# A two-layer adaLN transformer kernel: its beginning rearranged, and a maxima lead of 40 units for 46

## The reference

```python
q = qkv[..., :2 * Hx].reshape(Bx, 2 * NQ, Sx, HD)      # 32 query heads, 8 key heads
scores = where(causal, einsum('bhqd,bhkd->bhqk', q, k) / sqrt(HD), -inf)
aw = softmax(scores).reshape(Bx, NQ, 2, Sx, Sx)
attn = einsum('bhqk,bhkd->bhqd', aw[:, :, 0] - lam * aw[:, :, 1], v) * (1 - LAMBDA_INIT)
```

## Time and profile before

| | |
|---|---|
| Median of 3 runs | 2183.7 us (2183.66 to 2185.52) |
| The profiled execution's own time | 2184.72 us |
| Its span | 2183.0 us |
| Busy share of the span: TensorE, VectorE, ScalarE, GpSimd | 94%, 80%, 70%, 32% |
| Mean granted clock of TensorE | 0.973 of 2.4 GHz |
| Beginning, to the first maxima matmul | 0 to 66.07 us |
| Lead, to the first score matmul | to 115.41 us |
| 16 groups | to 1794 us |
| Layer 0's end and layer 1 | to 2183 us |

### The profile page before, as it was taken

The page is one execution under the profiler, slowest core; times in us unless marked ns, Lnnn a source line. Parts: engine busy times, 40 slices in busy tenths (PEclk is TensorE's granted clock), DMA queues, the critical chain, the costliest instruction groups (busy, mean ns, idle before and its releaser), DMA issues. The chain is left out here.

```text
span 2183.0 us, 44397 instructions
## 1 busy us (share of the span) xinstructions
PE 2043.1 (94%) x16332; PEld 890.0 (41%) x16332; DVE 1739.4 (80%) x3954; ACT 1523.4 (70%) x3113; POOL 693.0 (32%) x1246
## 2 busy tenths in 40 slices
PE   6799999999999999999999999999999998978896
PEld 5233333333333333333333333333333327855674
DVE  2888888888888888888888888888888926833688
ACT  2068787878787878787878778787867784523564
POOL 2213232414141414232333323242311213410577
PEclk9599999999999999999999999999999998989998
DMA  5230404040303131212222221312120003110111
GB/s 150 41 70 10 74 7 74 7 73 10 70 15 65 23 58 27 53 33 48 37 43 45 36 50 30 53 28 52 29 47 24 9 2 97 39 48 1 30 49 49
DMA packets 138229, 93.09 MB, mean 43 GB/s; under 512 B 90784, under 2 KB 127776, under 8 KB 138016
## 3 DMA queue, kind: packets, MB, share of 16 engines
q1 hardware_dynamic: 138016, 90.30, 20.4%
HBM read 31.00 MB, written 20.97 MB: 24 GB/s over the span
## 5 line engine op out<-in xcount | busy, mean ns | idle before, releaser
L758 ACT ACTIVATE probs<-b_bank 128x512 f32<-128x512 f32 (+1 forms) x2304 | 1172.4, 577 | 347.2 <-PE b_bank L918 336.4
L635 DVE TENSOR_REDUCE m_part<-a_bank 128x1 f32<-128x512 f32 (+3 forms) x2048 | 1190.1, 634 | 153.8 <-PE a_bank L888 109.8
L918 PE MATMUL b_bank<-q_pack,k_pack 34*128 34x512 bf16 (+7 forms) x5120 | 920.8, 347 | 3.9 <-DMA q_pack<-m_rows 2.2
L888 PE MATMUL a_bank<-k_pack,q_pack 64*128 64x512 bf16 (+3 forms) x2560 | 810.7, 357 | 54.8 <-DVE m_part L635 31.6
L960 PE MATMUL acc<-probs,v_tile 128*32 128x512 f32 (+3 forms) x5120 | 587.4, 540 | 3.1 <-POOL probs L501 0.8
L918 PEld LDWEIGHTS b_bank<-q_pack,k_pack 64*128 64x128 bf16 (+1 forms) x5120 | 310.3, 94 | 510.6 <-ACT probs L758 436.5
L888 PEld LDWEIGHTS a_bank<-k_pack,q_pack 64*128 64x128 bf16 x2560 | 226.0, 94 | 344.6 <-DVE m_part L635 210.6
L501 POOL TENSOR_SCALAR_AFFINE_SELECT probs<-probs 128x512 f32<-128x512 f32 (+1 forms) x192 | 152.2, 793 | 608.1 <-ACT probs L758 608.0
L632 DVE CUSTOM_DVE_ANT_0 a_bank<-a_bank,mask_a 128x128 f32<-128x128 f32 (+3 forms) x512 | 241.7, 512 | 66.8 <-PE a_bank L888 66.8
L960 PEld LDWEIGHTS acc<-probs,v_tile 128*32 128x32 f32 x5120 | 107.9, 108 | 175.5 <-issue 118.5
L516 POOL TENSOR_TENSOR o_w<-o_rl,signs 128x16 f32<-128x16 f32 x64 | 14.8, 232 | 413.6 <-DVE o_rl L658 413.6
(11 more groups left out here) (210 smaller groups left out, 1756.3 us busy)
## 6 DMA issues: line engine op xcount, KB each, us to landing
q_pack<-part SPq DMA_DIRECT2D x384, 64.0 KB, 2.3
k_pack<-part SPq DMA_DIRECT2D x192, 64.0 KB, 2.3
headT<-scratch SPq DMA_DIRECT2D x80, 128.0 KB, 4.0
scratch<-qkvT SPq DMA_DIRECT2D x16, 512.0 KB, 3.0
xg<-in_L_attn_x SPq DMA_DIRECT2D x16, 256.0 KB, 2.7
scratch<-qkvT SPq DMA_DIRECT2D x32, 128.0 KB, 2.9
q_pack<-m_rows SPq DMA_DIRECT2D x256, 2.0 KB
x<-in_L_attn_x SPq DMA_DIRECT2D x4, 1024.0 KB, 9.2
```

The costliest lines, as they stand in the source:

```text
L635: dve.tensor_reduce(out, bank[:, 0:w], AX.X, ALU.max).then_inc(a_maxed, 1)
L758: act.activation(probs[:, n % P_RING, h, at:C], b_bank[bank_no(("B", n, h))][:, at:C], ACT.Exp, scale=HD ** -0.5) \
L888: ins = pe.matmul(a_bank[at % A_RING][:, 0:w], q_pack[buf][rows, hp, 0, q:q + P], k_pack[buf][rows, 0, C * c:C * c + w], start=True, stop= ...
L918: ins = pe.matmul(b_bank[bank_no(slot)][:, at:at + C - q], k_pack[par][rows, n2, P * kt:P * (kt + 1)], q_pack[par][rows, h // 2, n2, C * j ...
```

## The change

LEAD goes from 46 to 40. On GpSimd the first power comes ahead of most constants. The 36 DMAs of the first packing are divided: SyncE issues those of side 0, ScalarE those of side 1, each behind the same conditions; later groups keep all on SyncE. The row modulations leave their place before the lead: their twelve halves follow units 13, 14, 16, 17, 19, 20, 29, 30, 32, 33, 35 and 36, and ScalarE copies them. The lambda computation moves up on VectorE and ScalarE.

```diff
@@ constants @@
-LEAD = 46
+LEAD = 40
...
+MODS_AT = {u + w: (n, w) for n, u in enumerate((13, 16, 19, 29, 32, 35)) for w in range(2)}
@@ new helpers @@
+        def part_made(p):
+
+            return ((part0_ready, PIECES), (rest_ready, 2 * ROUND_AT), (parts_ready, 1))[p]
+
+        def pack_part(queue, buf, p, sides):
+
+            for n2 in range(2):
+                for r, (pq, pk) in enumerate(zip(PARTS_Q[n2], PARTS_K[n2])):
+                    for side in sides:
+                        at = HALF * side + HD * r
+                        if pk == p:
+                            queue.dma_start(k_pack[buf][at:at + HD, n2, :], part[p][HD * QH:HD * (QH + 1), :]).then_inc(packs_in, 16)
+                        for h in range(side, QH if pq == p else 0, 2):
+                            queue.dma_start(q_pack[buf][at:at + HD, h // 2, n2, :], part[p][HD * h:HD * (h + 1), :]).then_inc(packs_in, 16)
@@ SyncE, pack(n, buf, steps_done) @@
                 for p in range(3):
                     if steps_done is None:
-                        sp.wait_ge(*((part0_ready, PIECES), (rest_ready, 2 * ROUND_AT), (parts_ready, 1))[p])
-                    for n2 in range(2):
...
+                        sp.wait_ge(*part_made(p))
+                    pack_part(sp, buf, p, range(2) if steps_done is not None else (0,))
@@ GpSimd: inverse_deviation and its call for 0 moved up, behind mask_a's select @@
+            def inverse_deviation(n):
...
+            inverse_deviation(0)
             made(pool.memset(pick[:, :, :], 0.0))
...
-            inverse_deviation(0)
             inverse_deviation(1)
@@ GpSimd, pair(n) @@
                 if n == 0:
                     pool.wait_ge(lam_step, 7)
+                    pool.wait_ge(mod_taken, len(ROW_MODS))
@@ VectorE: row copies out; the lambda block moved from behind them to behind centre(1) @@
             centre(1)
+            dve.wait_ge(lam_inputs, 64)
+            dve.tensor_tensor(products, lam_in[:, 0:4:2, :], lam_in[:, 1:4:2, :], ALU.mult).then_inc(lam_step, 1)
...
-            for n in range(6):
-                dve.wait_ge(mod_ready, upto(3 + n))
-                _, b, _, at = ROW_MODS[n]
-                dve.tensor_copy(rowmod[:, at:at + 2, b, :],
-                                (b_bank[0], acc)[n % 2][:, :].rearrange("p (w d) -> p w d", w=2)).then_inc(mod_taken, 1)
@@ ScalarE @@
+            act.wait_ge(lam_step, 2)
+            act.activation(lam[:, 2:4], lam[:, 0:2], ACT.Exp).then_inc(act_consts, 1)
             for i in range(PIECES):
                 first_part(0, i)
-            act.wait_ge(lam_step, 2)
-            act.activation(lam[:, 2:4], lam[:, 0:2], ACT.Exp).then_inc(act_consts, 1)
+            act.wait_ge(pool_consts, POOL_CONSTS)
+            for p in range(3):
+                act.wait_ge(*part_made(p))
+                pack_part(act, 0, p, (1,))
+
+            def take_row_mod(n):
+
+                act.wait_ge(mod_ready, 3 + n)
+                _, b, _, at = ROW_MODS[n]
+                act.activation(rowmod[:, at:at + 2, b, :], (b_bank[0], acc)[n % 2][:, :].rearrange("p (w d) -> p w d", w=2), ACT.Copy) \
+                    .then_inc(mod_taken, 1)
+
             take_maxima(0, N_PRO - 1)
+            for n in range(2):
+                take_row_mod(n)
             for i in range(PIECES):
                 first_part(1, i)
+            take_row_mod(2)
             take_maxima(1, N_PRO)
+            for n in range(3, 6):
+                take_row_mod(n)
@@ TensorE: the loop over ROW_MODS ahead of the lead becomes row_mod(n, w) @@
+            def row_mod(n, w):
+
+                layer, b, cols, _ = ROW_MODS[n]
+                if n >= 2 and w == 0:
+                    pe.wait_ge(mod_taken, n - 1)
+                for kc in range(2):
+                    ins = pe.matmul((b_bank[0], acc)[n % 2][:, D * w:D * (w + 1)], cSb[:, layer, kc, b, :],
...
@@ TensorE, in the loop over the lead's units @@
                     turn_maxima(m)
-
+                if u in MODS_AT:
+                    row_mod(*MODS_AT[u])
+
+            pe.wait_ge(mod_taken, len(ROW_MODS))
             pe.wait_ge(m_copied, len(NEXT))
```

More of the change, by code:

```diff
@@ L425, in _ @@
                                     pattern=[[-1, P]], channel_multiplier=1))
+            def inverse_deviation(n):
+                pool.wait_ge(stats_ready, upto(n + 1))
+                if not (isinstance(n, int) and n == 0):
+                    pool.wait_ge(xhat_ready, upto(n))
+                pool.tensor_tensor(rstd[:, :], veps[:, :], expo[:, 0:2], ALU.pow).then_inc(rstd_ready, 1)
+            inverse_deviation(0)
             made(pool.memset(pick[:, :, :], 0.0))
@@ L454, in _ @@
             pool.wait_ge(pool_consts, POOL_CONSTS)
[L456 to L460, removed]
             def split(n, i):
@@ L586, in _ @@
             centre(1)
+            dve.wait_ge(lam_inputs, 64)
+            dve.tensor_tensor(products, lam_in[:, 0:4:2, :], lam_in[:, 1:4:2, :], ALU.mult).then_inc(lam_step, 1)
+            dve.wait_ge(lam_step, 1)
+            dve.tensor_reduce(lam[:, 0:2], products, AX.X, ALU.add).then_inc(lam_step, 1)
+            dve.wait_ge(act_consts, 2)
+            dve.tensor_tensor(lam[:, 4:5], lam[:, 3:4], lam[:, 2:3], ALU.subtract).then_inc(lam_step, 1)
+            dve.wait_ge(lam_step, 3)
+            dve.tensor_scalar(lam[:, 5:6], lam[:, 4:5], -LAMBDA_INIT, 1.0 - LAMBDA_INIT, ALU.add, ALU.mult).then_inc(lam_step, 1)
+            dve.memset(lam[:, 6:7], 1.0 - LAMBDA_INIT).then_inc(lam_step, 1)
+            dve.wait_ge(lam_step, 5)
+            dve.tensor_copy(signs[:, :, 0:4:2], lam[:, 6:7].unsqueeze(1).broadcast_to([P, TB, 2])).then_inc(lam_step, 1)
+            dve.tensor_copy(signs[:, :, 1:4:2], lam[:, 5:6].unsqueeze(1).broadcast_to([P, TB, 2])).then_inc(lam_step, 1)
             for i in range(ROUND_AT):
@@ L868, in _ @@
             pe.wait_ge(silu_ready, 1)
[L869 to L878, removed]
+            def row_mod(n, w):
[4 more added lines that the diff above has]
+                    ins = pe.matmul((b_bank[0], acc)[n % 2][:, D * w:D * (w + 1)], cSb[:, layer, kc, b, :],
+                                    wmods[:, layer, kc, D * cols[w]:D * (cols[w] + 1)], start=kc == 0, stop=kc == 1)
+                    if n == w == kc == 0:
+                        ins.then_inc(pv_done, START)
+                if w == 1:
+                    ins.then_inc(mod_ready, 1)
             def unit_head(u, n):
```

## The result

The changed kernel takes 2246.2 us (median of 4 runs, 2245.6 to 2248.8) against 2183.9 us for the kernel before, run beside it: a ratio of 1.0286 with a 95% interval of 1.0268 to 1.0304. It is slower, as forecast, but by 62.3 us where 23.5 were forecast, and lies outside the range of 2180 to 2225. The profiled execution has a span of 2244.1 us and a mean granted clock of 0.965 (before 0.973).

A forecast was written before the change was run, and what follows sets the result against it. TensorE was taken to have no room in the 16 groups, so its waits there are lost sixteen times. Terms −4.5 − 11.4 + 8 − 6.7 + 1.3 + 36.8 = +23.5 gave 2208.2 us profiled, 2207 us; range 2180 to 2225.

The forecast's parts named there:

- early power: Beginning: GpSimd's first norm power ahead of its constants brings the turn of the rows forward, −4.5 us (bounds 0 and 6.4).
- two queues: Beginning: first packing's 36 DMAs issued by SyncE and ScalarE, 18 each, bring the first maxima matmul earlier, −11.4 us.
- a matmul about 2 us later: Packing: if a DMA share of 1.0 were the ceiling, first maxima matmul and sum would come about 2 us later.
- Row modulations: Inside the lead: twelve halves in two bursts, about 4 us lost per burst, +8 (bounds 0 and +18.5).
- Lead of 40: Before the groups: six fewer units let the loop begin 6.7 us earlier, −6.7.
- The six units in the last group: Last group: the units taken from the lead come back there at 0.22 us each, +1.3.
- The late turn: Every group: block 3's turn in step 19 makes step 21 wait 1.9 us; 2.3 per group, +36.8 (bounds 0, 54).
- Rival 2: Groups: each wait throws the clock down, 3.4 us per group, +54.4, 2225 us; chance 0.10.
- the units' places: Groups: rearranged units cost or save up to 0.4 us a group, ±6, taken as 0.
- (1): Groups absorb the wait and only the beginning counts: −13.3, 2170 us; chance 0.14.
- (3): Packing: ScalarE's DMA issues do not run beside SP's, 11.4 us back, 2219 us; chance 0.09.
- (4): Beginning: the early power does nothing because another wait replaces it, 4.5 us back, 2212 us; chance 0.05.

The follow-up runs named there:

- experiment 9: Changed kernel (lead 40) with block 3's turn one step earlier and the next group's block 0's turn one step later: 2184.5 us, ratio 0.9996.
- experiment 1: Changed kernel with LEAD back at 46, all else as changed: 2182.2 us against 2184.6, ratio 0.9985.
- experiment 3: Changed kernel, lead 40, with only block 3's maxima turn moved one step earlier: 2190.1 us, ratio 1.0027.
- experiment 7: Changed kernel with lead 46 and all row modulations ahead of the lead, in six idle banks, copied by VectorE: 2173.0 us, ratio 0.9946.
- experiment 2: Kernel before with LEAD 40 instead of 46 and nothing else: 2248.5 us, ratio 1.0287.
- Experiment 4: Kernel before, lead 46, with block 3's turn three steps later (step 19) and the next group's block 0's one later: 2221.0 us, ratio 1.0164.
- experiment 8: Changed kernel with a lead of 42 instead of 40, putting block 3's turn in step 18: 2205.9 us, ratio 1.0097.

## Why the prediction was wrong

**What bounds the kernel** held. TensorE has no room in a group, and no wait for maxima rows came back: 2.4 us idle cost 2.6 and more, 1.57 idle cost 1.75 and more. A shorter wait did come back in part: taking away the 0.88 us in step 22 (experiment 9) gained 0.32.

**Beginning.** The early power was forecast at −4.5; the runs show −3.7 alone and −5.6 in the profiled pair. Right. The two queues were forecast at −11.4 and gave −9.1 to −9.2. Two things differ. The issues were close to the 0.634 us assumed but not all: the last began 11.3 (SyncE) and 11.7 us (ScalarE) after the first instead of 10.8. And from ScalarE's last issue, at 47.5, to the first maxima matmul it is 3.7 us, not the 2.4 of the single queue; a DMA share of 1.24 in 48 to 51 us fits transfers that still ran side by side, though the value tile and the next group's heads, issued from 47.79 on, are in it as well. The prediction had gone by an earlier window with a share of 1.27, which was no licence to expect the full gain. By the Trainium skill (DMA: Bandwidth & Descriptors, Rules for kernel authors), which says that several issuing engines still share the 16 DMA engines, the estimate was a matmul about 2 us later; this case's runs agree in size, with 2.2, but not in the way there: that estimate took a steady share of 1.0, and the share was 0.82 over 36 to 48 us. That the shared engines are the cause was not tried by itself.

**Row modulations** were forecast at +8 and cost +11.7 (12.1 in experiment 1, 11.5 in experiment 9, 9.2 in the one and 11.6 in the other profiled execution of experiment 3, and nothing in experiment 7, where they lie ahead of the lead). The step that failed is "half the time at each level", read from a window ahead of the lead: in the changed kernel three of the six halves of each burst took 2.07 or 2.08 us and a fourth 1.5 or 1.6. The price of a half was low too: the prediction halved 3.78 us to 1.89, from products that run one behind the other, and a half between units takes 2.08. The twelve took 20.1 us by their rows, where 17.0 lies midway between the prediction's two bounds of 22.7 and 11.3. VectorE, which sets the lead's pace, was held up meanwhile: it is busy 40.55 of 54.3 us (75%), before 46.81 of 49.4 (95%).

**Lead of 40**: −6.7 forecast; experiment 2 shows −6.9. (By the prediction's own terms the first score matmul comes at 100.8, not near 100.6; it came at 105.50.) The six units in the last group: +1.3 forecast, +1.2 in experiment 3 (92.57 against 91.37). Right.

**The late turn** is the step that failed by its size: +36.8, bounds up to 54; the loop lost 71.1. By experiment 3 that is

- 55.9 for the wait with its clock (1749.7 against 1693.9 of the same kernel without the wait), 3.5 per group instead of 2.3. The chain from turn to landed rows was read correctly: 4.70 us in group 8, 5.0 forecast. But the prediction took the time between the turn and step 21 from a place of the old order, 3.1 us; in the new order it is 2.3, so the bare wait is 2.4 to 2.5 and not 1.9. (Experiment 4 has the late turn in the old order. In a second profiled execution of it the chain is 4.99 us in group 8 and the wait 1.56, so there 3.4 us stand between the turn and step 21.) On top, after some waits TensorE also idles 0.6 for ScalarE's exponentials at step 23, and in 9 of the first 14 groups the clock falls, 0.8 us per group on the mean. Rival 2, 3.4 per group, was nearer than the forecast's 2.3, but only partly for its reason: it had the clock fall in every group, and it fell in nine of 14. Of the 1.2 us missing in each group, 0.5 to 0.6 is the longer bare wait.
- 14.0 for the rest of the new order (15.2 in experiment 3, less the six units). Experiment 9's loop, 1688.3, splits it: 5.6 for the turn of the next group's block 0, now in step 22, whose negation is late, and 8.4 for the units' places. The prediction had asked of that turn only when its rows are needed, not whether its own input is ready, and had taken the places as 0, give or take 6. They cost more than that, and no row read before the result shows it; with a lead of 42 it was 1.8 us a group (experiment 8).

Of the other rivals: the groups absorbed nothing of the wait for rows (1), ScalarE's issues ran (3), the power counted (4). The direction was right because the largest term was found; the range failed because its neighbours had been read as a spread around zero, and all of them cost.

The terms together: of the 38.8 us missing, 19.1 are the wait, 14.0 the second turn and the units' places, 3.7 the row modulations and 1.1 the later first unit; 0.9 is left, within the scatter of single executions. The 1.1 is small by luck: in seven other profiled executions of kernels with the same beginning (experiments 1, 3, 7, 8 and 9) the first unit comes at 51.5 to 55.3, in five of them at 52.4 to 53.0, and not at 51.2.

## What to carry to other kernels

Where a planner spreads work by a lead, changing the lead moves every due point behind it. List each of these points and ask two things: when is its result needed, and is its own input there. A gain of 15 us at the beginning is worth less than one microsecond in a loop of 16 turns. And before work is moved into a stretch where TensorE "has room", look at which engine sets that stretch and whether it would wait for TensorE meanwhile: idle time beside a transfer was the better place.

## What the runs showed that was not expected

**The same idle time, with and without a fall of the clock.** In the changed kernel TensorE idles 2.42 to 2.48 us at step 21 in nearly every group. In groups 5, 8, 9, 12 and 13 the clock stays at 2.4 GHz behind it, and steps 20 to 24 take 16.32 us. In the other nine part of these steps runs at 1.2 GHz, and they come in runs in which the loss grows: 16.89, 17.64, 18.24 and 18.25 us in groups 1 to 4 (group 4 also idles longest, 2.79), then 17.05 and 17.95 in groups 6 and 7, then 16.96 and 17.75 in groups 10 and 11. Group 0 stands by itself with 17.87. Experiment 2 repeats the pattern, with falls in nine of the first 14 groups (0 to 4, 7, 8, 11 and 12). In a second profiled execution of this same kernel eight fall, and they are others: 0, 1, 3, 4, 7, 8, 12 and 13, with 2.44 to 2.49 us idle in all 14. With 1.57 us idle (experiment 4) 4 of 14 fall, every third (4, 7, 10 and 13), and lose 1.1 us; in its second execution group 3 falls too. So neither the length of the idle time nor the place in the program decides alone. That it matters where in time the idle stretch lies is a guess; against what was not tried.

**Ahead of the groups the clock is low even though TensorE works.** In experiment 7 the lead runs at 0.50 with TensorE busy 44.7 of 49.4 us, as before. With float32 products among the units it rises for a time (0.66 on the mean in the changed kernel, 0.64 in experiment 1), yet the lead is longer by the products' time.
